# A six-stage transformer kernel on one core: attention's bias products over 128 rows of the array, ranks and transposed rows taken one unit sooner

## The chip, the core and the metric

The kernel runs on one core of one Trainium2 chip. The core has a matmul engine (TensorE, "PE"; its weight loads are "PEld"), a vector engine (VectorE, "DVE"), a scalar engine (ScalarE, "ACT"), GpSimd ("POOL") and SyncE ("SP"), which here only issues DMAs. They run apart from one another and meet at semaphores. The metric is the device time of one execution in microseconds; lower is better.

## The reference

The input is x of shape 16 x 256 x 128, 4096 tokens of width 128. Six stages follow, each added to x. The one that the change touches is the second, a differential attention with 16 heads of width 8, two maps each:

```
x = x + 0.5 * ffn(layernorm(x))          # experts, top 2 of 8
x = x + attn(layernorm(x))               # the stage of the change
x = x + 0.5 * ffn(layernorm(x))          # experts again
x = x + 0.5 * quantized_ffn(layernorm(x))
x = x + linear_attention(layernorm(x))
x = x + 0.5 * quantized_ffn(layernorm(x))

attn: q = x @ Wq.T + bq; k = x @ Wk.T + bk; v = x @ Wv.T + bv; rope on q1, q2, k1, k2
      a1 = softmax(causal(q1 k1 * scale)); a2 = softmax(causal(q2 k2 * scale))
      out = (a1 - lam * a2) @ v, divided by its root mean square, times head_norm_w and 0.8
      return out @ Wo.T + bo
```

The third stage sorts tokens by expert. Its routing of a group of 512 tokens (normalise, transpose, router product, the two best experts, the rank of each token within its expert, the row it is sent to) is done inside the attention, for all groups but the last of eight.

## The kernel before

All of x stays in SBUF, as 32 tiles of 128 tokens. `diff_attention` works on 16 blocks of two tiles (256 tokens) in 19 turns, which this text numbers 0 to 18. In turn t, block A = t is projected and packed, block B = t-1 gets its scores for the row maxima, block C = t-2 its transposed scores, exponentials and value products, and block D = t-3 its division, normalisation and output product. A turn has 24 units u; each engine's program is written out unit by unit, and this order alone sets what runs when, as no scheduler moves anything. Between engines there are semaphores and buffers of two or six.

What the text refers to:

- In each unit PE computes `scores(B, u)` into one of two banks `s_ps` (L2202, L2205, L2210) and `scores_T(C, u)` into one of two banks `st_ps` (L2227). DVE takes the row maximum of `s_ps` (L1933, "the maximum of unit u"); PE may write scores of unit u only after the maximum of unit u-2. ACT takes the exponential of `st_ps` into `prob` (L1784), POOL clears its upper triangle (L1719, "select"), and in every second unit PE multiplies by the values with 32 columns of weights (L2250).
- Bias products: the bias is added by a matmul of its own, whose stationary operand `two_ones` has ones in rows 0 and 32 and zeros elsewhere, and whose moving operand holds the bias in its leading 16 bits in row 0 and the rest in row 32. For q, k and v (L2371) it stands in units 7 and 10, ahead of three projection matmuls (L2373), twice in each of these units (256 and 384 columns): "a pair". For the output product it stands in unit 15 (L2398), ahead of `wo` (L2399), twice.
- `m_ps`, two banks, is shared by all the small transposes and products, so PE's later users of it wait for the readers of the earlier. In unit 5 PE transposes `oT` into it (L2353); DVE then divides (L1941, L1944), squares and sums in unit 6 (up to L1957). POOL raises the sums to the power -1/2 (L1686, twice, units 7 and 8), DVE multiplies by it in unit 10 (L2132).
- Rope: DVE multiplies the projections by cosine and sine (L1970, L1972) in units 8 and 11, POOL adds the two (L1741, "rope addition") in units 9 and 12, ACT packs the result (L1838, L1841), DVE forms the low part of `k_pack` (L2164), PE transposes it (L2414) in unit 15.
- Transposed rows: in even turns from 6 to 16 PE transposes 512 normalised tokens into bank 1 of `m_ps` in unit 2 (L2268), and ACT copies them to `exp_xT` (L1805, 128 x 1024). PE's transposes of `oT` in unit 5 wait for that copy.
- Ranks: in odd turns from 7 to 17 PE computes the ranks into the same bank in unit 2 (L2283, L2285), and DVE's `take_ranks` adds them to `run` (L2040, L2042, the tile `exp_run`). PE's unit 5 waits for that too, and for `xT_lo` (L2153, unit 3 on DVE).
- POOL also sends rows to HBM by indirect DMA (L1707, "scatter"); in even turns from 8 on the first of them is in unit 5.

## Time and profile before

| | us |
|---|---|
| median of 3 runs | 1323.84 |
| lowest, highest | 1322.83, 1324.23 |
| the profiled execution | 1324.04 |
| its span in the trace | 1322.3 |

| engine | busy us | share |
|---|---|---|
| PE | 1092.7 | 83% |
| PEld | 819.8 | 62% |
| DVE | 985.9 | 75% |
| POOL | 856.6 | 65% |
| ACT | 724.3 | 55% |

A row of the timeline gives the start, the duration, engine, source line, operation, what is written and read, the sizes and a count, and in brackets how long the engine had been idle and which instruction released it. For a matmul, "64\*128 64x256" means that 64 rows and 128 columns of the array are used and 256 columns stream through. The end of a matmul is modelled: the distance between the starts of two of them tells more than their durations. In the timeline, neighbouring instructions of one group are merged (x2 and more). A brief idle time has no bracket. The granted clock of PE is 1.00 for 2.4 GHz and 0.50 for 1.2 GHz.

### The profile page before, as it was taken

To read this page: it belongs to the slowest core of one execution; us is meant where nothing else is said; L and a number is where in the kernel's file an instruction comes from. 1 tells how busy PE (TensorE), PEld (TensorE's weight loads), DVE (VectorE), ACT (ScalarE), POOL (GpSimd) and SP (SyncE) were. 2 spreads that over 40 slices of the span, in tenths; PEclk is the share of its full clock that TensorE was granted. 3 is DMA by queue.
4 is the path that set the end of the run, shared out by engine and by line. 5 is a ranking of instruction groups with operands and counts; after the bars stand their busy time and mean duration, and the time that the engine had idled before them with its cause. 6 is when DMAs were issued, how large, how long until landed. Compare 5 with 4: busy or idle time off the path is not lost. (4 is left out here: it accounts for less than half of the span.)

```text
span 1322.3 us, 32967 instructions
## 1 busy us (share of the span) xinstructions
PE 1092.7 (83%) x11805; PEld 819.8 (62%) x11805; DVE 985.9 (75%) x2554; ACT 724.3 (55%) x1311; POOL 856.6 (65%) x1033
## 2 busy tenths in 40 slices
PE   2753996389999999999999988579994988999697
PEld 1432775156666666666666665368883875777577
DVE  6872885588888888989898875378885936888672
ACT  4721554446667676667666676335662744444174
POOL 4874777225667688878787887544774315889651
PEclk9886998589999999999999999679997898999989
DMA  8113431011110011111011010143323100000001
GB/s 258 45 48 106 112 106 53 26 39 26 26 25 20 20 30 34 33 30 33 25 34 34 24 28 12 43 132 93 105 74 115 36 1 0 1 1 1 0 25 40
DMA packets 63980, 62.78 MB, mean 47 GB/s; under 512 B 11088, under 2 KB 53488, under 8 KB 63440
## 3 DMA queue, kind: packets, MB, share of 16 engines
q1 hardware_dynamic: 54384, 39.66, 11.4%
q0 software_dynamic: 9440, 21.02, 4.7%
q8 instruction: 99, 1.62, 0.5%
q14 instruction: 57, 0.47, 0.1%
HBM read 28.10 MB, written 24.17 MB: 40 GB/s over the span
## 5 line engine op out<-in xcount | busy, mean ns | idle before, releaser
L1784 ACT ACTIVATE diff_prob<-diff_st_ps 128x512 f32<-128x512 f32 x384 | 227.8, 601 | 160.9 <-PE diff_st_ps L2227 154.2
L1933 DVE TENSOR_REDUCE diff_q_pack<-diff_s_ps 128x2 f16<-128x512 f32 (+1 forms) x384 | 262.1, 692 | 63.5 <-PE diff_s_ps L2210 60.9
L1719 POOL TENSOR_SCALAR_AFFINE_SELECT diff_prob<-diff_prob 128x256 f32<-128x256 f32 (+1 forms) x384 | 188.0, 497 | 121.9 <-ACT diff_prob L1784 119.6
L431 POOL DMA_INDIRECT exp_ys<-moe_y_sb,moe_dest x156 | 152.7, 979 | 86.8 <-ACT moe_y_sb L514 54.1
L2210 PE MATMUL diff_s_ps<-diff_k_one,diff_qT 128*128 128x128 f16 (+1 forms) x1024 | 149.8, 249 | 0.0
L2227 PE MATMUL diff_st_ps<-diff_qmT,diff_k_one 128*128 128x256 f16 (+1 forms) x1024 | 147.7, 248 | 0.3 <-ACT diff_prob L1784 0.2
L2250 PE MATMUL diff_ot_ps<-diff_prob,diff_v 128*32 128x128 f32 x3072 | 125.5, 282 | 9.1 <-POOL diff_prob L1719 6.8
L507 ACT ACTIVATE moe_h_hi<-moe_h 128x512 f16<-128x512 f32 x94 | 59.2, 630 | 88.2 <-DVE moe_h L737 88.2
L1686 POOL TENSOR_TENSOR diff_rms<-diff_ms,all_neghalf 128x8 f32<-128x8 f32 x64 | 105.0, 1641 | 3.7 <-DVE diff_ms L1957 2.8
L2210 PEld LDWEIGHTS diff_s_ps<-diff_k_one,diff_qT 128*128 128x128 f16 x1024 | 90.7, 99 | 22.2 <-issue 0.7
L2250 PEld LDWEIGHTS diff_ot_ps<-diff_prob,diff_v 128*32 128x32 f32 x3072 | 73.3, 110 | 44.5 <-issue 23.3
L2551 POOL TENSOR_TENSOR lin_y<-lin_state,lin_qT 128x512 f32<-128x512 f32 x64 | 81.9, 1280 | 11.3 <-DVE lin_state L2694 8.9
L2227 PEld LDWEIGHTS diff_st_ps<-diff_qmT,diff_k_one 128*128 128x128 f16 x1024 | 83.0, 98 | 8.8 <-ACT diff_prob L1784 2.0
L2694 DVE TENSOR_TENSOR_SCAN lin_state<-lin_lam_ps,lin_kv 128x512 f32<-128x512 f32 x64 | 77.6, 1219 | 9.3 <-POOL lin_kv L2538 7.5
L414 POOL DMA_INDIRECT exp_xs<-moe_xh,exp_rows x64 | 66.8, 1044 | 23.8 <-issue 19.0
L501 ACT ACTIVATE moe_act<-moe_g_ps 128x512 f32<-128x512 f32 x94 | 55.8, 593 | 45.9 <-PE moe_g_ps L957 41.6
L2765 PEld LDWEIGHTS lin_o_ps<-last_lin_wo,lin_y 128*128 128x128 f32 x512 | 64.9, 191 | 22.1 <-POOL lin_y L2551 18.9
L2202 PE MATMUL diff_s_ps<-diff_mask,diff_ident_bf 128*128 128x256 bf16 x256 | 72.1, 282 | 7.5 <-DVE diff_q_pack L1933 5.4
L2765 PE MATMUL lin_o_ps<-last_lin_wo,lin_y 128*128 128x128 f32 x512 | 70.2, 280 | 9.0 <-POOL lin_y L2551 8.4
L737 DVE TENSOR_TENSOR moe_h<-moe_act,moe_u_ps 128x512 f32<-128x512 f32 x94 | 64.4, 686 | 15.2 <-PE moe_u_ps L957 14.3
L732 DVE TENSOR_TENSOR moe_h_lo<-moe_h,moe_h_hi 128x512 f16<-128x512 f32 x94 | 65.1, 692 | 10.2 <-ACT moe_h_hi L507 9.0
L718 DVE COPY moe_xgT<-moe_t_ps 128x512 f16<-128x512 f16 x78 | 33.0, 424 | 38.9 <-PE moe_t_ps L939 37.7
(390 smaller groups left out, 3069.8 us busy)
## 6 DMA issues: line engine op xcount, KB each, us to landing
moe_xg<-exp_xs SPq DMA_DIRECT2D x78, 130.0 KB, 2.3
diff_k_one<-diff_kT SPq DMA_DIRECT2D x128, 64.0 KB, 2.0
diff_yg<-exp_ys SPq DMA_DIRECT2D x14, 256.0 KB, 3.0
fetched_yg<-exp_ys SPq DMA_DIRECT2D x7, 512.0 KB, 3.9
exp_ys<-moe_y_sb,moe_dest POOLq DMA_INDIRECT x156
all_x<-in_x SPq DMA_DIRECT2D x4, 512.0 KB, 5.1
moe_up<-in_w SPq DMA_DIRECT2D x16, 128.0 KB, 3.9
out<-all_x SPq DMA_DIRECT2D x8, 256.0 KB, 2.3
```

The costliest lines, as they stand in the source:

```text
L431: nc.gpsimd.indirect_dma_start(out=ew.ys, out_offset=bass.IndirectOffsetOnAxis(ap=dest[:, s, j:j + 1], axis=0), in_=y_sb[:, s % YR, j], in ...
L1686: nc.gpsimd.tensor_tensor(rms[:, j, heads], ms[:, j, heads], neghalf[:, 0:8], ALU.pow).then_inc(rms_ready, 1)
L1719: nc.gpsimd.affine_select(out=pr, in_=pr, compare_op=ALU.is_ge, fill=0.0, base=0, pattern=[[0, n], [1, P]], channel_multiplier=-1).then_in ...
L1784: nc.scalar.activation(prob[:, u % RING], st_ps[:, u % 2], ACT.Exp, scale=SCALE).then_inc(exp_ready, 1)
L1933: nc.vector.tensor_reduce(q_pack[:, par, j, m0:m0 + n, 3 * HD], s_ps[:, u % 2].rearrange("p (m k) -> p m k", m=n), op=ALU.max, axis=AX.X, ...
L2202: nc.tensor.matmul(out.rearrange("p (m k) -> p m k", k=P)[:, 1::2], ident_bf[:], mask[:, 0:2], start=True, stop=False, skip_group_check=True)
L2210: last = nc.tensor.matmul(out[:, i * wd:(i + 1) * wd], qT[:, par, c, j * P:(j + 1) * P], k_one[:, par, r, c, 0:wd], start=False, stop=True ...
L2227: last = nc.tensor.matmul(st_ps[:, u % 2, i * wd:(i + 1) * wd], k_one[:, par, r, c, key * P:(key + 1) * P], qmT[:, par, c, q0:q0 + wd], st ...
L2250: last = nc.tensor.matmul(ot_ps[32 * r:32 * r + 32, c // 2, col:col + P], v[:, par, key, (m0 + i) // 2], src, start=bool(key) and c % 2 == ...
L2551: nc.gpsimd.tensor_tensor(y[:, f % RING], state[:, f % STATES], qT[:, b], ALU.mult).then_inc(y_ready, 1)
L2694: nc.vector.tensor_tensor_scan(state[:, f % STATES], lam_ps[:, b], kv[:, f % RING], 0.0, ALU.mult, ALU.add).then_inc(state_ready, 1)
L2765: last = nc.tensor.matmul(o_ps[:, b, t * P:(t + 1) * P], y[:, f % RING, t * P:(t + 1) * P], wo[:, f], start=(f == 0 and t == 0), stop=(f = ...
```

## The change

`bias_rows`, `two_ones` and `wo_rows` get 128 partitions instead of 64, and the copies that fill them cover all 128. Rows 64 to 127 of `two_ones` are cleared with the rest, so the added products are zero times the bias. `take_ranks` moves from unit 4 to unit 3 on DVE, the copy to `exp_xT` from unit 4 to unit 3 on ACT. In unit 3 `take_ranks` stands ahead of `xT_lo`. The whole diff:

```diff
@@ -1496,9 +1496,9 @@
         xn = nm.sb("xn", [P, 2, P], F32)
         xT_hi = nm.sb("xT_hi", [P, S], F16)
         xT_lo = nm.sb("xT_lo", [P, S], F16)
-        bias_rows = nm.sb("bias_rows", [2 * LO, QKV], F16)
-        two_ones = nm.sb("two_ones", [2 * LO, P], F16)
-        wo_rows = nm.sb("wo_rows", [2 * LO, P], F16)
+        bias_rows = nm.sb("bias_rows", [P, QKV], F16)
+        two_ones = nm.sb("two_ones", [P, P], F16)
+        wo_rows = nm.sb("wo_rows", [P, P], F16)
         v_new = nm.sb("v_new", [P, 2, HEADS, HD], F32)
         v = nm.sb("v", [P, 2, 2, HEADS, PACK], F32)
         by_cos = nm.sb("by_cos", [P, 2, 2 * MAPS, HD], F32)
@@ -1799,7 +1799,7 @@
                             if norms >= 2:
                                 a.wait_ge(scattered[norms % 2], norms // 2 * 2 * TG * 16)
                             nc.scalar.activation(ew.xh[:, norms % 2, :, 0:P], n_xn[:], ACT.Copy).then_inc(n_hi, 1)
-                    g = routes if u == 4 and places is None else norms if u == 21 and norms == routed - 1 else None
+                    g = routes if u == 3 and places is None else norms if u == 21 and norms == routed - 1 else None
                     if g is not None:
                         a.wait_ge(n_xT_in_psum, g + 1)
                         nc.scalar.activation(ew.xT[:, g].rearrange("p a n -> p (a n)"), m16[1], ACT.Copy).then_inc(n_xT_ready, 1)
@@ -1889,7 +1889,7 @@
                 once(nc.vector.memset(two_ones[:], 0.0))
                 for row in (0, LO):
                     nc.vector.memset(two_ones[row:row + 1], 1.0)
-                once(nc.vector.tensor_copy(bias_rows[:], qkv_bias[0:2 * LO]))
+                once(nc.vector.tensor_copy(bias_rows[:], qkv_bias[:]))
                 nc.vector.tensor_tensor(bias_rows[LO:2 * LO], qkv_bias[LO:2 * LO], bias_rows[LO:2 * LO],
                                         ALU.subtract).then_inc(prepared, 1)
 
@@ -1904,7 +1904,7 @@
                 nc.vector.tensor_copy(ident_bf[:], ident[:])
                 nc.vector.tensor_copy(mask[:], later.causal[:].unsqueeze(1).broadcast_to([P, 4, P]))
                 nc.vector.tensor_scalar(wo[:], later.diff_wo[:], head_w[:, 0:1], 1.0 - LAMBDA_INIT, ALU.mult, ALU.mult)
-                once(nc.vector.tensor_copy(wo_rows[:], wo_bias[0:2 * LO]))
+                once(nc.vector.tensor_copy(wo_rows[:], wo_bias[:]))
                 nc.vector.tensor_tensor(wo_rows[LO:2 * LO], wo_bias[LO:2 * LO], wo_rows[LO:2 * LO], ALU.subtract)
                 if routed:
                     nc.vector.memset(going[:, :, 1:], 1.0)
@@ -2073,7 +2073,7 @@
 
                 if u == 0:
                     mark_either(g)
-                if u == 4:
+                if u == 3:
                     take_ranks(g)
                 if u == 5:
                     place_pairs(g)
```

In the preparation on DVE, in turn 0, the names are the three widened operands and the biases as loaded:

```order
-L1889 MEMSET diff_two_ones 64x64
+L1889 MEMSET diff_two_ones 128x64
 L1891 MEMSET diff_two_ones 1x128 x2
-L1892 CAST diff_bias_rows<-later_qkv_bias 64x640
+L1892 CAST diff_bias_rows<-later_qkv_bias 128x640
 L1893 TENSOR_TENSOR diff_bias_rows<-later_qkv_bias,diff_bias_rows 32x640
```

Three instructions (the third is L1907) cover twice the partitions; none is added. PE's order is the same throughout, with 128 rows in L2371 and L2398.

On ACT, around unit 3 of turn 6 (and of every even turn up to 16), `diff_xT_hi` is the projection's input, `diff_oT` the copied value products, `diff_prob` the exponentials and `exp_xT` the transposed rows:

```order
 L1813 ACTIVATE diff_xT_hi<-diff_m_ps 128x256
 L1779 ACTIVATE diff_oT<-diff_ot_ps 128x512
-L1784 ACTIVATE diff_prob<-diff_st_ps 128x512 x2
+L1784 ACTIVATE diff_prob<-diff_st_ps 128x512
 L1805 ACTIVATE exp_xT<-diff_m_ps 128x1024
-L1784 ACTIVATE diff_prob<-diff_st_ps 128x512 x5
+L1784 ACTIVATE diff_prob<-diff_st_ps 128x512 x6
```

The copy passes the exponential of unit 4.

On DVE, around unit 3 of turn 7 (and of the later odd turns), `diff_q_pack` is written by the maxima, and `exp_xh` and `diff_placed` by the step that follows the ranks:

```order
 L2113 COPY diff_oT<-diff_ot_ps 128x512
 L1933 TENSOR_REDUCE diff_q_pack<-diff_s_ps 128x2
-L2153 TENSOR_TENSOR diff_xT_lo<-diff_m_ps,diff_xT_hi 128x256
-L1933 TENSOR_REDUCE diff_q_pack<-diff_s_ps 128x2
 L2040 TENSOR_TENSOR diff_base<-diff_m_ps,exp_run 128x32
 L2042 TENSOR_TENSOR exp_run<-exp_run,diff_m_ps 128x8
-L1933 TENSOR_REDUCE diff_q_pack<-diff_s_ps 128x2
+L2153 TENSOR_TENSOR diff_xT_lo<-diff_m_ps,diff_xT_hi 128x256
+L1933 TENSOR_REDUCE diff_q_pack<-diff_s_ps 128x2 x2
 L2045 TENSOR_REDUCE exp_xh<-diff_rest 128x4
 L2047 TENSOR_TENSOR diff_placed<-diff_chosen,diff_base 128x64
```

The two instructions on the ranks pass one maximum and `xT_lo`.

## Rows read from the trace of the kernel before

**Rows 1.** the page's first part: busy us, share of the span, instructions

```profile
PE 1092.7 (83%) x11805; PEld 819.8 (62%) x11805; DVE 985.9 (75%) x2554; ACT 724.3 (55%) x1311; POOL 856.6 (65%) x1033
```

**Rows 2.** busy us of each engine in turn 8, granted PE clock, DMA

```profile
494.60:530.20 35.60, 33.08 (x455) 23.49 (x456) 30.82 (x71) 23.96 (x43) 27.53 (x40) 1.00 0.12 32
```

**Rows 3.** PE timeline, turn 8, unit 10: start us, us, operation

```profile
...
509.22 0.28 PE L2371 MATMUL diff_m_ps<-diff_bias_rows,diff_two_ones 64*128 64x256 f16 x1
509.43 0.28 PE L2373 MATMUL diff_m_ps<-diff_wqkv_hi,diff_xT_hi 128*128 128x256 f16 x1
509.55 0.27 PE L2373 MATMUL diff_m_ps<-diff_wqkv_lo,diff_xT_hi 128*128 128x256 f16 x1
509.66 0.27 PE L2373 MATMUL diff_m_ps<-diff_wqkv_hi,diff_xT_lo 128*128 128x256 f16 x1
509.87 0.33 PE L2371 MATMUL diff_m_ps<-diff_bias_rows,diff_two_ones 64*128 64x384 f16 x1
510.13 0.34 PE L2373 MATMUL diff_m_ps<-diff_wqkv_hi,diff_xT_hi 128*128 128x384 f16 x1
510.31 0.33 PE L2373 MATMUL diff_m_ps<-diff_wqkv_lo,diff_xT_hi 128*128 128x384 f16 x1
...
```

**Rows 4.** releasers of the `oT` transposes L2353: us, times

```profile
...
  ACT exp_xT L1805: 3.5, 6
  DVE exp_run L2042: 3.2, 5
...
```

**Rows 5.** ACT timeline, turn 8, units 3 to 6

```profile
...
499.53 1.14 ACT L1784 ACTIVATE diff_prob<-diff_st_ps 128x512 f32<-128x512 f32 x2
500.57 1.02 ACT L1805 ACTIVATE exp_xT<-diff_m_ps 128x1024 f16<-128x1024 f16 x1
...
503.50 0.60 ACT L1784 ACTIVATE diff_prob<-diff_st_ps 128x512 f32<-128x512 f32 x1 [1.41 <-PE diff_st_ps L2227]
...
```

**Rows 6.** DVE timeline, maximum of unit 6 in turns 6, 9, 15, 16

```profile
...
433.34 0.70 DVE L1933 TENSOR_REDUCE diff_q_pack<-diff_s_ps 128x2 f16<-128x512 f32 x1 [0.60 <-PE diff_s_ps L2210]
...
538.81 0.68 DVE L1933 TENSOR_REDUCE diff_q_pack<-diff_s_ps 128x2 f16<-128x512 f32 x1
...
750.03 0.70 DVE L1933 TENSOR_REDUCE diff_q_pack<-diff_s_ps 128x2 f16<-128x512 f32 x1 [0.66 <-PE diff_s_ps L2210]
...
784.84 0.70 DVE L1933 TENSOR_REDUCE diff_q_pack<-diff_s_ps 128x2 f16<-128x512 f32 x1 [1.49 <-PE diff_s_ps L2210]
...
```

**Rows 7.** POOL timeline, turn 8, units 3 to 12

```profile
...
501.83 1.09 POOL L1719 TENSOR_SCALAR_AFFINE_SELECT diff_prob<-diff_prob 128x512 f32<-128x512 f32 x2
...
504.47 1.07 POOL L1707 DMA_INDIRECT exp_xs<-exp_xh,exp_rows  x1 [0.18 <-issue]
...
508.33 1.62 POOL L1686 TENSOR_TENSOR diff_rms<-diff_ms,all_neghalf 128x8 f32<-128x8 f32 x1
...
510.30 1.25 POOL L1741 TENSOR_TENSOR diff_by_cos<-diff_by_cos,diff_by_sin 128x512 f32<-128x512 f32 x1
...
514.14 1.27 POOL L1741 TENSOR_TENSOR diff_by_cos<-diff_by_cos,diff_by_sin 128x512 f32<-128x512 f32 x1 [0.92 <-DVE diff_by_sin L1972]
...
```

**Rows 8.** timeline, L2132 on DVE and L1741 on POOL, turns 4, 5, 8

```profile
...
371.20 1.26 POOL L1741 TENSOR_TENSOR diff_by_cos<-diff_by_cos,diff_by_sin 128x512 f32<-128x512 f32 x1
371.48 1.26 DVE L2132 TENSOR_TENSOR diff_osq<-diff_o,diff_rms 128x256 f32<-128x256 f32 x1
...
405.83 0.52 DVE L2132 TENSOR_TENSOR diff_osq<-diff_o,diff_rms 128x256 f32<-128x256 f32 x1
...
406.05 1.44 POOL L1741 TENSOR_TENSOR diff_by_cos<-diff_by_cos,diff_by_sin 128x512 f32<-128x512 f32 x1
...
510.35 1.85 DVE L2132 TENSOR_TENSOR diff_osq<-diff_o,diff_rms 128x256 f32<-128x256 f32 x1
...
```

**Rows 9.** DVE timeline behind bias pairs, turns 0 and 2

```profile
...
250.97 0.69 DVE L1970 TENSOR_TENSOR diff_by_cos<-diff_m_ps,later_rope_cos 128x512 f32<-128x512 f32 x1 [3.12 <-PE diff_m_ps L2373]
...
299.60 0.70 DVE L1933 TENSOR_REDUCE diff_q_pack<-diff_s_ps 128x2 f16<-128x512 f32 x1 [1.02 <-PE diff_s_ps L2210]
...
```

## The prediction, made before the changed kernel was run

> **What bounds the kernel now.** The page's first part gives the largest busy share to TensorE (PE) [rows 1], but that is a mean over six stages and the change lies in one of them, the attention of 240 to 852 us. Its 19 turns are numbered 0 to 18 here; turns 3 to 15 hold all four blocks and last about 35 us each. In turn 8 PE is busy for 33.08 of 35.60 us and VectorE (DVE) for 30.82 us, at a granted clock of 1.00, the 2.4 GHz level [rows 2]; the other full turns look alike. Neither bounds the whole turn, so I read the timeline of both engines beside each other. From unit 16 of a turn to unit 5 of the next, DVE and ScalarE (ACT) wait for PE. From unit 6 to unit 15 PE waits for DVE, or GpSimd (POOL) is late. A saving on PE is kept only where DVE next waits for PE.
>
> **Part 1, bias products over 128 rows.** The matmuls keep their columns; only the row count goes from 64 to 128. In [rows 3] equal full-array matmuls of 256 columns start 0.12 and 0.11 us apart (509.43, 509.55, 509.66). The 256-column bias matmul of 64 rows holds the next one off for 0.21 us (509.22 to 509.43), a full matmul holds the second bias matmul off for 0.21 us (509.66 to 509.87), and the 384-column bias matmul holds its successor for 0.26 us where its equal takes 0.18 (510.13 to 510.31). So each change between 64 and 128 rows costs PE about 0.10 us, and a pair of bias matmuls holds three that can go: 0.3 us. The change into the first stays wherever a 32-column value product stands ahead, or is hidden in a wait. The output product (unit 15) has four, 0.4 us. There are 32 pairs and 16 output products: 9.6 + 6.4 = 16.0 us of PE, of which most lies where PE waits anyway. Bounds for one change: 0, if the row count is not what holds the successor, and 0.10 us. I take 0.10, since the same pair shows the gap on both sides of the bias matmul. The one-time copies and the clearing on DVE cover more partitions but no more elements in each; I cost them at nothing.
>
> The Trainium skill (TensorEngine Tiling, Key Properties) says that changing the tiling mode drains TensorE; by that, the trace agrees. It gives no price there. TensorE: Matmul & The Clock Gate (Single matmul latency) puts the part of a lone matmul that does not depend on its columns at 398 cycles of 2.4 GHz, an estimate of 0.17 us for an exposed drain; a pair would then save 0.5 us and the whole sum would be some 1.5 us more. The 0.10 us of the rows decides.
>
> Where a pair's 0.3 us is kept: turn 0, where DVE waits 3.12 us for the second pair [rows 9], 0.4 us at the slower clock there; both pairs of turn 1, 0.6; turn 2, where DVE waits 1.02 us after the pair of unit 7 [rows 9], 0.3. The output product is bare in turn 16 (0.3) and in the last turn (0.35). In turns 3 to 15 the maximum of unit 8 waits some 0.2 us for PE's scores behind the pair of unit 7, but that gain meets POOL below. The output product in those turns is followed by the k_pack transposes, which wait for DVE: nothing.
>
> **Part 2, transposed rows one unit sooner (even turns 6 to 16).** ACT copies `exp_xT` at 500.57, for 1.02 us, behind two exponentials [rows 5]. PE's transposes of `oT` in unit 5 wait for it: 3.5 us in 6 turns [rows 4]. The copy now goes between the two exponentials and ends about 0.55 us sooner. The second exponential, that of unit 4, then ends 1.0 us later, at about 501.7. PE needs it for scores_T of unit 6. The exponential of unit 6 starts on that product's end, at 503.50 [rows 5]; 0.58 us sooner and less about 0.4 us for the product, scores_T would start at 502.5, so 0.8 us are to spare. POOL works on the two selects of units 3 and 4 from 501.83 [rows 7], and reaches the second at about 502.4, later than 501.7 too. So the delay costs nothing; with both covers gone it would cost up to 1.0 us a turn. What is late next: in turn 6 DVE waits 0.60 us for PE at the maximum of unit 6, in turn 16 it waits 1.49 us [rows 6]. Both keep 0.58 us: 1.2 us together. In turns 8, 10, 12 and 14 POOL has a scatter of 1.07 us in unit 5 and no wait for another engine ahead of the second power (508.33 to 509.95) and the rope addition at 510.30 [rows 7]: it runs by its own length. PE's and DVE's lead of 0.4 to 0.9 us (0.2 to 0.58 from the copy, 0.2 to 0.3 from the pair) does not move that POOL work. It moves DVE's L2132 against the rope addition L1741, and the two disturb each other [rows 8]: started 0.05 us after L1741, L2132 takes 1.85 us; 0.28 us after, 1.26 us; 0.22 us before, 0.52 us. With its lead L2132 waits only for the second power (509.95) and gets in ahead of 510.30. DVE's chain is then over 1 us sooner, and what ends it next is POOL, which waits 0.92 us for DVE before its second rope addition [rows 7]. I take that whole wait as the gain, 0.9, 0.9, 0.9 and 0.7 us in the four turns (the last has the shortest such wait): 3.4 us. Bounds: 0, if L2132 still falls behind L1741, and 1.3 us a turn.
>
> The Trainium skill (Advanced Engine Details and Errata, GPSIMD Details) says that GpSimd shares a read and a write interface with VectorE, in conflict with its instructions of two SBUF inputs. L2132 has two such inputs; by that, the trace agrees, and the rows give the price that the page lacks.
>
> In turns 3 and 4 L2132 starts 0.28 us after L1741 [rows 8]. The 0.2 us that the pair gives there brings it to some 0.08 us after, where 1.85 us stands instead of 1.26: the end is tied to L1741, and I count a loss of 0.35 us each, 0.7 us. Turn 5 has L2132 ahead already and gains 0.2. Turn 6 could fall either way: 0.
>
> **Part 3, ranks one unit sooner (odd turns 7 to 17).** PE's unit 5 waits 3.2 us in five turns for `exp_run` [rows 4]. The two DVE instructions (0.18 and 0.16 us) now stand ahead of `xT_lo`, which is 0.36 us later within its unit but still ahead of the maximum of unit 4; its end then releases PE, some 0.6 us sooner. But in turn 9 the maximum of unit 6 starts at 538.81 with no wait for PE [rows 6], right behind DVE's own work, and turns 7, 11 and 13 are alike: nothing is kept. In turn 15 no fetched tile is added, DVE waits 0.66 us [rows 6], and 0.6 us is kept. Turn 17 has no such PE wait. No wait, DMA or queue of SP moves; POOL's order is unchanged.
>
> **The sum.** Starts 0.4 + 0.6 + 0.3 = 1.3; turns 3 to 6 -0.7 + 0.2 = -0.5, and 0.58 for turn 6; turns 8 to 14 3.4; turn 15 0.6; turn 16 0.58 + 0.3; turn 18 0.35. Together 6.6 us. Against the profiled execution of 1324.04 us (span 1322.3) that is 1317.4; this execution lies 0.2 us above the median of 1323.84, so 1317.2, rounded to 1317.3.
>
> **The rivals.** (a) L2132 does not get ahead of L1741 in the four turns, because what DVE wins is used up before unit 10. For it: POOL's own work does not move. Against: the lead is 0.4 us or more and 0.05 us is enough. It costs the 3.4 us: 1320.7; with half of the terms of turns 6, 15 and 16 (2.1 us) gone too, 1321.7. (b) PE bounds more than I read: the whole 16.0 us and the 6.7 us of unit 5 are kept, 1301; half of them kept gives 1312.5. Against: PE's waits for DVE between units 11 and 15. (c) The row change does not shorten the gaps (the part does not do what it says): 2.15 us of starts, ends and turn 5 go and the 0.7 us loss too, 1318.7. (d) Slower: the new timing puts L2132 within 0.09 us after L1741 in all full turns. The place is unit 10, the price 0.59 us where 1.26 stands now (7 turns) and 1.35 us where about 0.5 stands (2 turns): 6.8 us, and the 3.4 us never come. Against 3.2 us of other gains that is 3.6 us slower, 1327.4. It decides at the start of L1741: a start just after it is dear, one just before it is cheap. Against: the second power ends 0.35 us ahead of L1741.
>
> **How the numbers follow.** Forecast 0.50; (a) 0.27, two thirds of it with the further losses; (b) 0.10, nearly all in its halved form; (c) 0.07; (d) 0.06. A measurement of this kernel tells about 0.2% from no change; the bound is 1321.2 us. Faster by more: 0.50 + 0.09 of (a) + 0.10 + 0.07 = 0.76; within 0.2%: the 0.18 left of (a); slower: 0.06. The range reaches over (c), nearly all of (a) and about the halved (b): 1311.0 to 1322.0. It leaves out (d), the full (b) and the tail of (a).
>
> **What would show it.** Bias matmuls of 128 rows with successors 0.11 and 0.17 us behind them; no PE wait at the transposes of unit 5 for `exp_xT` or `exp_run`; L2132 near 0.5 us in turns 8 to 14 and near 1.8 in turns 3 and 4; odd turns 7 to 13 as long as before, even turns 8 to 14 about 0.9 us shorter. The forecast is wrong if the even turns do not shrink, or if the odd ones shrink as well.

## The result, and the profile after

The changed kernel takes 1319.34 us (median of 8 runs, 1316.73 to 1322.09) beside 1324.03 us of the kernel before (8 runs, 1322.75 to 1324.86): ratio 0.997, interval 0.9961 to 0.9978, so 3 to 5 us faster. The forecast was 1317.3 us with a range of 1311.0 to 1322.0. The page's first part, to set beside [rows 1]:

```profile
PE 1070.2 (81%) x11758; PEld 821.9 (62%) x11805; DVE 986.0 (75%) x2554; ACT 725.3 (55%) x1311; POOL 857.2 (65%) x1033
```

PE's modelled busy time falls by 22 us (47 of its 11805 records are missing here) and no other engine's changes by over 2.1 us; the kernel kept some 4. PE's timeline of the bias pair in turn 8, unit 10 (start us, us, operation), beside [rows 3]:

```profile
506.96 0.27 PE L2371 MATMUL diff_m_ps<-diff_bias_rows,diff_two_ones 128*128 128x256 f16 x1
507.06 0.27 PE L2373 MATMUL diff_m_ps<-diff_wqkv_hi,diff_xT_hi 128*128 128x256 f16 x1
...
507.28 0.27 PE L2373 MATMUL diff_m_ps<-diff_wqkv_hi,diff_xT_lo 128*128 128x256 f16 x1
507.39 0.33 PE L2371 MATMUL diff_m_ps<-diff_bias_rows,diff_two_ones 128*128 128x384 f16 x1
507.55 0.33 PE L2373 MATMUL diff_m_ps<-diff_wqkv_hi,diff_xT_hi 128*128 128x384 f16 x1
```

The bias matmuls hold their successors off for 0.10 and 0.16 us, where [rows 3] had 0.21 and 0.26, and the full matmul ahead of the second one holds it off for 0.11. The three gaps of 0.10 us are gone. In the output product of the same turn the four gaps that could go gave 0.48 us together. What L2353 waits for, beside [rows 4] (us, times):

```profile
  issue: 1.7, 6
  DVE diff_oT L2113: 1.5, 1
  DVE diff_logits L2020: 1.1, 1
```

`exp_xT` and `exp_run` no longer stand there. So parts 1, 2 and 3 do at their own places what they say. Turn 8 as a window, beside [rows 2], 35.30 us; from the first L2300 of one turn to that of the next it is 35.30 against 35.52 before:

```profile
493.00:528.30 35.30, 31.67 (x451) 23.50 (x454) 30.90 (x71) 23.88 (x43) 27.79 (x40) 1.00 0.12 32
```

PE works 1.41 us less there and the turn is 0.22 us shorter. L2132 on DVE and L1741 on POOL, in turns 3, 5 and 8 of the changed kernel, beside [rows 8]:

```profile
336.25 1.48 DVE L2132 TENSOR_TENSOR diff_osq<-diff_o,diff_rms 128x256 f32<-128x256 f32 x1
336.19 1.27 POOL L1741 TENSOR_TENSOR diff_by_cos<-diff_by_cos,diff_by_sin 128x512 f32<-128x512 f32 x1
...
405.31 0.61 DVE L2132 TENSOR_TENSOR diff_osq<-diff_o,diff_rms 128x256 f32<-128x256 f32 x1
405.62 1.44 POOL L1741 TENSOR_TENSOR diff_by_cos<-diff_by_cos,diff_by_sin 128x512 f32<-128x512 f32 x1
...
508.44 1.92 DVE L2132 TENSOR_TENSOR diff_osq<-diff_o,diff_rms 128x256 f32<-128x256 f32 x1 [0.21 <-POOL diff_rms L1686]
508.75 1.27 POOL L1741 TENSOR_TENSOR diff_by_cos<-diff_by_cos,diff_by_sin 128x512 f32<-128x512 f32 x1
```

In turn 8 L2132 gets its lead of 0.31 us, as forecast, and takes 1.92 us, not 0.5. In turn 5 the same lead gives 0.61.

The table has the stretches of the profiled executions, us. A turn runs from its first L2300 to the next turn's; turns 0 and 1 from the first L2313, 17 and 18 to the first L972, the experts from there to the last L972, the rest to the end of the span. "odd" is turns 7, 9, 11, 13 together, "even" 8, 10, 12, 14. The runs marked * were made on a chip on which the stages ahead of and behind the attention are longer (the kernel before takes 1417.47 us there); their attention turns are to be compared all the same, since the turns without a change agree to 0.05 us. Of the runs without a mark, before again and the three kernels with L2132 in unit 11 were made on one chip, the changed kernel again and parts 1, 2 and 3 alone on another.

| kernel | 0–1 | 2 | 3–5 | 6 | odd | even | 15 | 16 | 17–18 | experts | rest |
|---|---|---|---|---|---|---|---|---|---|---|---|
| before | 50.65 | 31.34 | 102.52 | 34.93 | 140.04 | 141.80 | 34.73 | 31.11 | 46.88 | 145.0 | 323.1 |
| before, again | 51.54 | 31.34 | 102.48 | 34.93 | 140.04 | 141.77 | 34.73 | 31.11 | 46.16 | 144.5 | 323.0 |
| changed | 50.94 | 30.94 | 102.10 | 34.29 | 139.44 | 141.05 | 36.22 | 30.56 | 43.76 | 147.2 | 323.3 |
| changed, again | 49.55 | 30.93 | 102.08 | 34.29 | 139.38 | 143.10 | 34.65 | 30.56 | 43.86 | 144.8 | 322.6 |
| part 1 alone | 49.77 | 30.93 | 102.06 | 34.76 | 139.39 | 145.01 | 34.70 | 30.62 | 43.76 | 147.2 | 323.6 |
| part 2 alone | 50.33 | 31.35 | 102.51 | 34.58 | 140.04 | 140.85 | 34.72 | 32.26 | 44.16 | 147.2 | 323.3 |
| part 3 alone | 50.35 | 31.34 | 102.53 | 34.93 | 140.63 | 141.93 | 34.66 | 31.12 | 44.01 | 145.2 | 323.0 |
| L2132 in unit 11 | 49.77 | 30.93 | 101.16 | 33.73 | 138.59 | 138.78 | 34.69 | 30.72 | 45.63 | 147.1 | 323.3 |
| and odd scatters | 49.66 | 30.93 | 101.60 | 33.93 | 138.52 | 138.68 | 34.14 | 30.18 | 45.86 | 146.8 | 322.6 |
| and unit-5 scatter | 49.61 | 30.92 | 101.12 | 33.73 | 138.41 | 135.53 | 34.12 | 29.94 | 44.92 | 144.7 | 322.6 |
| parts 1 and 2 * | 50.10 | 30.94 | 102.11 | 34.48 | 139.45 | 143.14 | 34.72 | 30.56 | 44.50 | | |
| L1741 in unit 10 * | 49.80 | 30.20 | 100.35 | 33.62 | 139.20 | 146.65 | 34.66 | 30.56 | 44.26 | | |
| odd scatters * | 49.26 | 30.93 | 102.11 | 34.30 | 140.06 | 142.56 | 33.47 | 30.56 | 45.15 | | |
| both * | 49.66 | 30.20 | 99.74 | 33.61 | 136.53 | 148.89 | 33.49 | 30.56 | 44.72 | | |

### The profile page after: what moved, and what is told of

The parts are those of the page before. It is cut to its first block and busy times, and to the rows that moved or that the text cites. A ratio compares the mean times of both kernels' runs of the same rounds, so it can differ in the third digit from the quotient of the medians.

```text
span 1319.7 us, 32920 instructions
## 1 busy us (share of the span) xinstructions
PE 1070.2 (81%) x11758; PEld 821.9 (62%) x11805; DVE 986.0 (75%) x2554; ACT 725.3 (55%) x1311; POOL 857.2 (65%) x1033
## 5 line engine op out<-in xcount | busy, mean ns | idle before, releaser
L2227 PE MATMUL diff_st_ps<-diff_qmT,diff_k_one 128*128 128x256 f16 (+1 forms) x1024 | 147.2, 247 | 0.3 <-ACT diff_prob L1784 0.2
L2250 PEld LDWEIGHTS diff_ot_ps<-diff_prob,diff_v 128*32 128x32 f32 x3072 | 73.3, 110 | 45.9 <-issue 21.1
```

Of the source, the lines that this page charges most:

```text
L2227: last = nc.tensor.matmul(st_ps[:, u % 2, i * wd:(i + 1) * wd], k_one[:, par, r, c, key * P:(key + 1) * P], qmT[:, par, c, q0:q0 + wd], st ...
L2250: last = nc.tensor.matmul(ot_ps[32 * r:32 * r + 32, c // 2, col:col + P], v[:, par, key, (m0 + i) // 2], src, start=bool(key) and c % 2 == ...
```

## The experiments

### The changed kernel again, and the kernel before again

> The changed kernel once more, for a second profile of it on another run of the chip. What is asked: does turn 15 again lose about 1.5 us against the kernel before, with PE waiting 1.8 us ahead of the k_pack transposes L2414 at unit 15 and its granted clock at 0.50 in the 2 us behind it, and does turn 17 again run at 1.00 where the kernel before ran at 0.50? If the fall of the clock belongs to the program (theory: the wait of 1.8 us is long enough by itself), both come again, turn 15 at 36.2 us and the whole at 1319.3 plus or minus 1. If it is a matter of where the chip happens to look (rival), turn 15 comes out at about 34.7 us in this profile and the runs spread over 5 us again.

Measured: 1319.71 us (6 runs). Turn 15 took 34.65 us, so the loss of the first profile did not come again; turns 10 and 14 were 0.7 and 1.5 us longer than in the first profile instead. Turn 14 is thus one kernel in one turn on two executions. PE is the same up to its wait for `by_sin` in unit 13; here are windows of 2 us (PE, PEld, DVE, ACT, POOL busy, granted clock, DMA), the changed kernel first, then again:

```profile
722.00:724.00 2.00, 1.38 (x27) 1.12 (x29) 1.96 (x5) 1.41 (x4) 1.28 (x1) 1.00 0.00 0
724.00:726.00 2.00, 1.88 (x29) 1.44 (x29) 1.54 (x4) 2.00 (x5) 0.64 (x1) 1.00 0.03 8
```

```profile
724.00:726.00 2.00, 1.80 (x21) 1.56 (x21) 1.40 (x4) 1.92 (x5) 1.33 (x2) 0.54 0.00 0
726.00:728.00 2.00, 2.00 (x28) 1.28 (x25) 1.32 (x4) 2.00 (x5) 0.84 (x2) 0.61 0.03 8
```

Behind the same two waits of PE (1.15 us for DVE's maximum, 0.62 us for `by_sin`) the clock stayed at 1.00, the 2.4 GHz level, in one execution and fell to 0.5, the 1.2 GHz level, in the other. The falls shown here stand behind such waits, but the same waits come without a fall too. The expected theory that the wait of 1.8 us in turn 15 is enough by itself is wrong: it came again, 1.83 us at L2414, and the clock stayed at 1.00. The experts' stage shows the same: 32 to 48 us into it the clock was 0.69 and 0.88 in the first profile and 0.79 and 1.00 in the second, and the stage took 147.2 and 144.8 us:

```profile
881.20:889.20 8.00, 6.36 (x47) 5.29 (x48) 7.62 (x23) 2.39 (x4) 0.00 (x0) 0.69 0.50 119
889.20:897.20 8.00, 8.00 (x93) 7.46 (x92) 6.76 (x19) 3.48 (x6) 0.00 (x0) 0.88 0.21 51
```

```profile
882.70:890.70 8.00, 7.54 (x70) 6.59 (x71) 7.63 (x24) 1.98 (x4) 0.00 (x0) 0.79 0.47 116
890.70:898.70 8.00, 7.95 (x99) 7.15 (x97) 7.73 (x22) 3.99 (x8) 0.00 (x0) 1.00 0.29 69
```

> The kernel before once more, for a second profile. From the first L2300 of turn 17 to the first L972 behind the attention the profile of before has 46.92 us; the profiles of the changed kernel, of it again, and of parts 1, 2 and 3 alone have 43.81, 43.86, 43.76, 44.16 and 44.0. If the missing 3 us are one execution's fall of the granted clock (0.50 through 825 to 830 us), as part 3 alone says, which hardly differs from before there, this profile shows about 44 us and a clock of 0.9 or more in that stretch, with the turns before it as in the first profile to 0.1 us. If the change gained them (rival), it shows 46.9 again. On whatever chip it runs, the turns' lengths are to be the same to 0.1 us, except where the clock fell.

Measured: 1323.78 us (11 runs), ratio 0.9995 (0.9986 to 1.0004). Turns 17 and 18 took 46.16 us, against 46.88 in the first profile. That is not the 44 us of the theory, and it is not clearly the rival either: the twelve profiles of other kernels lie between 43.8 and 45.9, and the three of them that were made on the same chip as this one have 45.63, 45.86 and 44.92, while the four on the chip of parts 1, 2 and 3 have 43.76 to 44.16. Those three kernels differ from the changed one in these turns too, so the chip's part in it is not separated. In before's two profiles, in the changed kernel's two and in part 3 alone PE waits 2.7 us for POOL's select in turn 17 and the clock falls to 0.50 at about that wait. PE then runs at 1.2 GHz for some 10 and 7 us in before's two profiles, for some 3 us in the changed kernel's first and in part 3 alone, and for some 7 us, the first of them within the wait, in the changed kernel's second, which took 43.86 us all the same. Before, two windows:

```profile
820.00:826.00 6.00, 4.65 (x49) 3.25 (x49) 1.30 (x2) 3.13 (x7) 5.62 (x9) 0.56 0.05 14
826.00:832.00 6.00, 6.00 (x54) 4.08 (x54) 2.17 (x6) 2.32 (x5) 2.88 (x6) 0.58 0.07 22
```

and part 3 alone, whose work is the same there up to that wait:

```profile
821.40:827.40 6.00, 4.67 (x53) 3.40 (x54) 1.30 (x2) 3.10 (x7) 5.62 (x9) 0.72 0.05 14
827.40:833.40 6.00, 5.65 (x96) 3.76 (x93) 3.27 (x9) 4.46 (x8) 5.47 (x9) 1.00 0.10 33
```

Part 3 alone, which saves nothing ahead of that wait, has the gain too, so the saved work does not make it. What sets the length of the low clock stays open, and so does whether more executions would keep before and the others apart.

### Each part alone

Part 1 alone (against the changed kernel):

```diff
-                    g = routes if u == 3 and places is None else ...
+                    g = routes if u == 4 and places is None else ...
...
-                if u == 3:
+                if u == 4:
                     take_ranks(g)
```

> Part 1 alone: bias matmuls over 128 rows, transposed rows and ranks at unit 4 as before. By the prediction's own terms: starts 1.3, turns 3 to 5 -0.5, ends 0.65, and of the four even turns nothing or little: 1.5 to 2.2 us faster than before. What the trace of after suggests instead: turns 0 to 2 1.1 us, turns 3 and 4 nothing (L2132 takes 1.48 us there, not 1.85), the last three turns up to 3 us of clock and gaps: 2.5 to 4 us faster, so that this part alone carries most of the 4.7 us. Rival (PE bounds all): 16 us faster or a good part of it. The bias matmuls must show successors 0.11 and 0.17 us behind them, and PE's waits for exp_xT (3.5 us a turn) and exp_run (3.2) in unit 5 must still be there, 0.3 to 0.5 us longer.

Measured: 1325.46 us (12 runs) beside 1323.53 (29 runs), ratio 1.0011 (1.0 to 1.0023): no gain at all, for the part that saves PE 16 us. In its profile turns 0 to 2, 3 to 5, the odd turns and the last two did gain (by the table 1.7, 0.4, 0.65 and 2.8 us against the mean of before's two), and the even turns gave 3.2 back, the experts 2.5. PE's waits in unit 5 are still there, 3.5 us for `exp_xT` and 3.2 for `exp_run`. Turn 12:

```profile
649.35 3.03 DVE L2132 TENSOR_TENSOR diff_osq<-diff_o,diff_rms 128x256 f32<-128x256 f32 x1
...
649.16 0.40 POOL L1719 TENSOR_SCALAR_AFFINE_SELECT diff_prob<-diff_prob 128x256 f32<-128x256 f32 x1
649.53 1.26 POOL L1741 TENSOR_TENSOR diff_by_cos<-diff_by_cos,diff_by_sin 128x512 f32<-128x512 f32 x1
650.76 1.34 POOL L1719 TENSOR_SCALAR_AFFINE_SELECT diff_prob<-diff_prob 128x256 f32<-128x256 f32 x3
654.32 1.27 POOL L1741 TENSOR_TENSOR diff_by_cos<-diff_by_cos,diff_by_sin 128x512 f32<-128x512 f32 x1 [2.23 <-DVE diff_by_sin L1972]
```

L2132 starts 0.18 us ahead of L1741, within a select, and ends at 652.38, 0.28 us behind the three selects (650.76 to 652.10) that follow L1741. It was held off through five POOL instructions, four of which started after it. PE then waits for DVE's maximum, and its clock falls:

```profile
653.05 0.28 PE L2202 MATMUL diff_s_ps<-diff_mask,diff_ident_bf 128*128 128x256 bf16 x1 [1.95 <-DVE diff_q_pack L1933]
```

```profile
654.00:656.00 2.00, 1.61 (x25) 1.31 (x29) 1.88 (x4) 1.73 (x5) 1.27 (x1) 0.81 0.00 0
656.00:658.00 2.00, 2.00 (x24) 1.40 (x25) 1.32 (x5) 2.00 (x6) 0.70 (x2) 0.50 0.03 8
```

Turn 12 is 1.67 us longer than before, turn 14, where L2132 takes 3.03 us again, 2.01. In turns 8 and 10 L2132 starts 0.01 us behind L1741, takes 1.53 us, and the turns gain 0.24 us each.

Part 2 alone (the kernel before with `u == 3` in ACT's copy of `exp_xT`):

> Part 2 alone: exp_xT copied in unit 3 of the even turns, bias products over 64 rows and ranks at unit 4 as before. By the prediction: turns 6 and 16 keep 0.58 us each, turns 8 to 14 gain up to 0.9 each if the lead of about 0.4 us brings L2132 ahead of L1741: 1.2 to 4.6 us faster. By the trace of after (a lead of 0.31 us did not shorten L2132, it took 1.92 us and ended 0.34 us behind L1741): 0.58 us in turns 6 and 16 and 0 to 0.15 in turns 8 to 14: 1.0 to 1.6 us faster. Rival: the second exponential, 1.0 us later, is waited for by POOL's select and PE's scores_T, and the turns get up to 0.5 us longer: 0 to 3 us slower.

Measured: 1321.91 us (12 runs), ratio 0.999 (0.998 to 0.9999): 1.6 us, just clear of no change. Turn 6 keeps 0.35, the even turns 0.95 together, and turn 16 loses 1.15: there L2132 stands beside POOL's selects alone, no L1741 is near. Part 2 first, then part 3 alone, turn 16:

```profile
790.28 1.92 DVE L2132 TENSOR_TENSOR diff_osq<-diff_o,diff_rms 128x256 f32<-128x256 f32 x1 [1.48 <-POOL diff_rms L1686]
...
790.22 1.70 POOL L1719 TENSOR_SCALAR_AFFINE_SELECT diff_prob<-diff_prob 128x256 f32<-128x256 f32 x4
```

```profile
792.92 0.61 DVE L2132 TENSOR_TENSOR diff_osq<-diff_o,diff_rms 128x256 f32<-128x256 f32 x1 [1.28 <-POOL diff_rms L1686]
...
792.86 1.89 POOL L1719 TENSOR_SCALAR_AFFINE_SELECT diff_prob<-diff_prob 128x256 f32<-128x256 f32 x4
```

Both L2132 start 0.06 us behind the first select. Once, in part 3 alone, DVE gets in behind the first select, and POOL's four selects take 0.19 us more; once, in part 2, it waits for all four. So the selects too, not the rope addition alone, shut it out.

Part 3 alone (the kernel before with `u == 3` ahead of `take_ranks`):

> Part 3 alone: ranks taken in unit 3 of the odd turns, bias products over 64 rows and transposed rows at unit 4 as before. By the prediction odd turns 7 to 13 keep nothing and turn 15 keeps 0.6 us: 0.6 us faster, no difference that can be measured. Rival: PE's wait of 3.2 us for exp_run is what holds the odd turns, then each of five gives up to 0.6 us: 3 us faster. Second rival: xT_lo, 0.36 us later, or the changed distance at the k_pack transposes of turn 15 costs: turn 15 longer by up to 1.5 us because PE idles 1.8 us there and its granted clock falls; if this part makes that, turn 15 is 36.2 us here, and 34.7 us in the kernel with part 1 alone.

Measured: 1323.72 us (11 runs), ratio 1.0002 (0.9993 to 1.001). Odd turns 7, 9 and 11 are as before to 0.01 us, turn 15 is 0.07 shorter; turn 13 is 0.58 longer in this profile, because DVE's L1926 waits 0.19 us for the DMA that fetches `diff_yg` and it and its neighbours then run later and longer. PE's shorter wait is given to DVE's own work, as the prediction had it for the odd turns.

Parts 1 and 2 without 3 (the changed kernel with `u == 4` ahead of `take_ranks`):

> The change without its third part: bias products over 128 rows and transposed rows in unit 3, ranks in unit 4 as before. Part 1 alone was 1.9 us slower than before in the median, with L2132 at 3.03 us in turns 12 and 14 (it had started 0.18 us ahead of L1741), part 2 alone 1.6 us faster, part 3 alone 0.2 us slower; their sum is 0.5 us slower, the whole change 4.3 us faster. Theory (part 2's lead moves L2132 in the even turns from 0.18 us to 0.31 us ahead of L1741, where it takes 1.92 us, and so takes part 1's loss away): 1318.5 to 1320.5, L2132 at 1.92 us in turns 8 to 14, and part 3 is worth nothing here either. Rival (part 3 is what makes up the difference): 1323 or more, with L2132 at 3.03 us in one or more of the even turns, or with odd turns 7 to 13 0.3 us longer than in the changed kernel.

Measured, on the other chip: ratio 0.9958 (0.9942 to 0.9975), 7 runs. L2132 takes 1.91 us in all four even turns, starting 0.31 us ahead of L1741, and of turns 2 to 16 none but turn 6 (34.48 for 34.29) and turns 10 and 14 (35.90 and 36.68 us, to 0.01 us as in the changed kernel's second profile, where the clock fell) differs from the changed kernel's undisturbed ones by over 0.1 us. Theory right: part 3 is worth 0.3 us at most, and parts 1 and 2 together are worth more than their sum, since part 2's lead moves L2132 from where it takes 3.03 us to where it takes 1.9.

### The price of the meeting

POOL's first rope addition one unit later (against the changed kernel):

```diff
-                        if u in (9, 12):
-                            j = (u - 9) // 3
+                        if u in (10, 12):
+                            j = (u - 10) // 2
```

> The changed kernel with one more edit: POOL does its first rope addition (L1741, 1.27 us) behind the select of unit 10 instead of unit 9, so that DVE's multiply L2132 no longer meets it. It measures the disputed cost by itself. Theory (the meeting of L2132 with L1741 is what uses up the lead of DVE and PE): L2132 takes 0.42 to 0.65 us in every turn instead of 1.28 to 1.93; turns 8, 10, 12 and 14 get up to 0.74 us shorter (that is POOL's wait for DVE before its second rope addition, which then ends the stretch), turns 3, 4 and 6 up to 0.8; odd turns 7 to 13 little, since POOL's second rope addition stands behind a scatter of 1.08 us there and does not wait for DVE: 3 to 6 us faster than the changed kernel, 1313 to 1316. Rival (POOL, or PE between units 11 and 15, bounds those units in all turns whatever L2132 does): no turn changes by over 0.1 us, 1319.3. Second rival: the first rope addition, 0.4 us later, delays ScalarE's k_pack and q_pack copies and PE idles longer before L2414: slower than the changed kernel by up to 0.4 us a turn.

Measured: ratio 0.9967 (0.9951 to 0.9983), that of the changed kernel, so no gain. By turns, against the changed kernel: 0.9 us gained in turns 3 and 4 each and 0.67 in turn 6, where L2132 now takes 0.60 us instead of 1.48; nothing in turn 5, where it had 0.61 before; 0.24 in each of turns 7, 9 and 13 (turn 11 is 0.5 longer, with DVE waiting for `diff_yg`); and 3.6 to 5.6 lost in the even ones together, the falls of the clock in turns 10 and 14 included. Turn 2, which has no L2132, gained 0.73 too, so L1741's place has a worth of its own and the price of the meeting is not measured cleanly. In the even turns L2132 starts 0.67 us ahead of L1741 and takes 2.57 us, through two selects, L1741 and the select behind it. The theory fails there: even a lead of 0.67 us is not enough.

The scatters of the odd turns later:

```diff
-    SEND_AT = {0: (10, 13, 16, 18, 19, 20, 22, 23), 4: (5, 16, 18, 20)}
+    SEND_AT = {0: (13, 16, 18, 19, 20, 21, 22, 23), 4: (5, 16, 18, 20)}
```

> The changed kernel with the scatters that POOL issues in odd turns moved from units 10, 13, 16, 18 to units 13, 16, 18, 19 (in turn 17 eight of them from 10 to 23 to 13 to 23), so that no scatter of 1.08 us stands ahead of its second rope addition. Theory on turn 15 (PE waits 1.83 us before L2414 because POOL's second rope addition is late behind the scatter; that wait lets the granted clock fall to 0.50 and costs 1.5 us): the wait falls to about 0.8 us, the clock stays at 1.00 through 760 to 768 us, turn 15 takes 34.7 us or less instead of 36.2. Odd turns 7 to 13, where L2164 waits 0.45 us for the k_pack copy behind that rope addition: up to 0.45 us shorter each. Together up to 3 us faster than the changed kernel, 1316.5. Rival (odd turns are bounded by DVE's own work there, and the fall of the clock comes with the wait at another place): within 0.5 us of 1319.3.

Measured: ratio 0.9976 (0.9961 to 0.9992), so the whole shows no gain over the changed kernel. Turn 15 takes 33.47 us, 1.2 less than the 34.65 of the undisturbed profile of the changed kernel. PE's wait in unit 15 there, the changed kernel and then this one:

```profile
761.22 0.91 PE L2414 MATMUL diff_m_ps<-diff_ident_h,diff_k_pack 128*128 128x128 f16 x8 [1.83 <-DVE diff_k_pack L2164]
```

```profile
809.59 0.62 PE L2414 MATMUL diff_m_ps<-diff_ident_h,diff_k_pack 128*128 128x128 f16 x8 [0.72 <-DVE diff_k_pack L2164]
```

So turn 15 is held by POOL's scatter of 1.08 us ahead of its second rope addition. Odd turns 7 to 13 gained nothing (140.06; turn 13 was 0.6 longer, with the same wait for `diff_yg` as in part 3 alone): rival right there.

Both edits:

> Both edits on the changed kernel: first rope addition in unit 10, scatters of the odd turns from unit 13 on. If L2132's meeting with L1741 (1.28 us instead of 0.5) and the scatter are two covers of the same stretch in the odd turns, each alone gives the odd turns little and both together give up to 0.7 us in each of turns 7, 9, 11, 13: 1310 to 1314 in all, faster than the sum of the two runs alone. If PE or DVE's other work bounds the odd turns, this is the sum of the two.

Measured: ratio 0.9944 (0.9924 to 0.9964), against 0.9967 and 0.9976. The odd turns fall to 136.53 us, 0.7 a turn below the changed kernel, where the edits alone gave 0.24 a turn and nothing: two covers of one stretch, as expected, that is, two pieces of work side by side, of which each hides most of what taking the other away would save. The even turns are at 148.89, so the whole misses the 1310 to 1314 that was expected (0.9944 would be 1316.6). There L2132 takes 2.57 us, PE waits 1.80 us for DVE, and the clock falls, turn 8:

```profile
548.45 2.57 DVE L2132 TENSOR_TENSOR diff_osq<-diff_o,diff_rms 128x256 f32<-128x256 f32 x1 [0.22 <-POOL diff_rms L1686]
```

```profile
551.69 0.28 PE L2202 MATMUL diff_s_ps<-diff_mask,diff_ident_bf 128*128 128x256 bf16 x1 [1.80 <-DVE diff_q_pack L1933]
```

```profile
550.00:552.00 2.00, 0.31 (x3) 0.29 (x4) 2.00 (x3) 0.00 (x0) 1.51 (x3) 1.00 0.00 0
552.00:554.00 2.00, 1.38 (x21) 1.12 (x20) 2.00 (x5) 1.08 (x3) 1.03 (x1) 0.69 0.00 0
554.00:556.00 2.00, 2.00 (x23) 1.26 (x21) 0.88 (x3) 2.00 (x6) 0.87 (x2) 0.50 0.00 0
```

### L2132 behind the meeting instead of ahead of it

Against the changed kernel, in DVE's program:

```diff
                     if D is not None:
-                        if u == 10:
+                        if u == 11:
                             dve.wait_ge(rms_ready, D * 4 + 4)
```

> The changed kernel with DVE's multiply L2132 taken in unit 11 instead of 10, behind that unit's maximum and ahead of the rope products; everything else, L1741's place too, stays. Theory (L2132 ends 0.28 us behind L1741 whenever it meets it, and what counts is what it holds up meanwhile): it starts 0.6 to 0.9 us later, takes 0.7 to 1.0 us and ends where it ended, but the maximum of unit 11 (0.6 us) is no longer held up behind it. So DVE's rope products and POOL's second L1741 come 0.6 us sooner: turns 3, 4, 6, 8, 10, 12 and 14 get 0.4 to 0.6 us shorter, odd turns 7 to 13 up to 0.2, since a scatter stands ahead of POOL's second L1741 there: 2.5 to 4.5 us faster than the changed kernel. Rival (POOL does not let L2132 in before its selects are through, as in part 1 alone, where it took 3.03 us, and with L1741 moved, 2.57 us): it takes 1.5 us or more in turns 8, 10, 12 and 14, these turns get longer, up to 1.9 us where PE's wait lets the granted clock fall to 0.50, and the whole is slower than the changed kernel.

Measured: 1316.07 us (5 runs), ratio 0.9927 (0.9914 to 0.9941): below the changed kernel by 3.6 us in the medians, by 5.3 in the ratios (0.9967 there). The even turns are 0.5 to 0.6 us shorter than the changed kernel's, the odd ones 0.2, turn 6 is 0.56, turns 3 and 4 0.6 and 1.0; turn 5, where L2132 had got in and now takes 1.05, is 0.66 longer. Theory right on the turns; L2132 takes 1.18 us in the even ones, where 0.7 to 1.0 was expected, and ends 0.34 us behind L1741. Turn 8:

```profile
507.98 1.18 DVE L2132 TENSOR_TENSOR diff_osq<-diff_o,diff_rms 128x256 f32<-128x256 f32 x1
...
507.56 1.26 POOL L1741 TENSOR_TENSOR diff_by_cos<-diff_by_cos,diff_by_sin 128x512 f32<-128x512 f32 x1
```

With the odd scatters later as well:

> The same with the scatters of the odd turns from unit 13 on. With L1741 moved and the scatters too, odd turns 7 to 13 were 0.83 to 0.90 us shorter than before, with the scatters alone 0.15. Theory: the two hold the same stretch of the odd turns, so this one has them 0.7 to 0.9 us shorter than before (0.6 to 0.7 shorter than the changed kernel), and even turns as in the run with L2132 in unit 11 alone: 5 to 7 us faster than the changed kernel. Rival (L2132's place is not what L1741's move was): odd turns 0.15 us shorter than before, and no more than 1.5 us in all over the run with L2132 in unit 11 alone, all of it in turn 15, whose wait before L2414 goes.

Measured: 1315.61 us (5 runs), ratio 0.9923 (0.9909 to 0.9936). The rival holds: the odd turns stay at 138.52, and the whole is the same as in the run before; turns 15 and 16 gain 0.55 us each, turns 4 and 6 lose 0.4 and 0.2. L2132 takes 0.68 us in the odd turns and ends 0.64 behind L1741, which itself stands where it stood; with both edits it took 0.41 ahead of an L1741 one unit later. Which of the two the odd turns' 2 us hang on was not tried.

And the scatter of unit 5 in the even turns later, `4: (16, 18, 19, 20)`:

> And the scatter of unit 5 in the even turns moved behind unit 16 too (units 16, 18, 19, 20 instead of 5, 16, 18, 20), so that POOL's two powers and its first rope addition come 1.08 us sooner there. Theory (in the even turns POOL's own work from unit 3 to unit 9 sets when L2132 may start): even turns 8 to 14 up to 0.9 us shorter than in the run without this edit, 1 to 3.5 us in all. Rival (the prediction's row: DVE and PE are next in line by 0.2 to 0.6 us): L2132 starts earlier but the turns gain 0.3 us or less, or, with POOL's selects in one piece behind it, L2132 takes 2.5 us or more again and they lose.

Measured: 1308.37 us (4 runs, 1308.03 to 1309.13), ratio 0.9878 (0.9863 to 0.9893). This version beats both kernels, by 16 and 11 us. The even turns fall from 138.68 to 135.53, 0.8 us each; theory right. In this run L2132 meets only the last 0.12 us of L1741 and POOL is 1.08 us sooner, both at once; which of the two gives the 0.8 us was not tried. Turn 8, with L2132 at 0.41 us:

```profile
507.32 0.41 DVE L2132 TENSOR_TENSOR diff_osq<-diff_o,diff_rms 128x256 f32<-128x256 f32 x1
...
506.17 1.27 POOL L1741 TENSOR_TENSOR diff_by_cos<-diff_by_cos,diff_by_sin 128x512 f32<-128x512 f32 x1
```

```profile
491.10:525.10 34.00, 31.86 (x455) 23.48 (x455) 29.39 (x72) 23.92 (x43) 27.66 (x40) 1.00 0.13 33
```

Turn 8 is 1.6 us shorter than before with the same work. The whole gained more than the even turns: of the 9.3 us between the two profiles 3.2 lie in them, 2.1 in the experts' stage (144.7 for 146.8), 1.9 ahead of the attention, 1.0 in turns 17 and 18, and 0.7 in turns 4 and 6. What the edit does there, if anything, is not shown; in the experts' stage it is the clock's matter again.

## Why the prediction was right, and where it was not

The time came within 2.1 us of the forecast and inside the range, but half of its sum did not happen, and other terms took its place. It lies nearer to rival (a), 1320.7, than to the forecast, and my own sign of being wrong came true: the even turns hardly shrank, and the odd ones shrank as well. "Gain" is the change against the two profiles of before.

**Row changes, 0.10 us each.** Right, to 0.01 us in the pairs; the output product gave 0.12 for each.

**Starts, 1.3 us.** Turn 2 gains 0.40 in every profile, for 0.3. Turns 0 and 1 gain 0.9 us in the mean of two profiles each, for 1.0, but the profiles of one kernel differ there by 0.9 and 1.4 us; over all, the ten with part 1 have 49.26 to 50.94, the four without it 50.33 to 51.54, and the means are 0.9 apart. So this term is supported, not shown.

**"With its lead L2132 ... gets in ahead", 3.4 us.** This step failed. L2132 got the lead and took 1.92 us. The even turns gained 0.22, 0.29, 0.16 and 0.08 us, 0.75 together, in the first profile (and lost 1.3 in the second, where the clock fell). I read [rows 8] as a matter of which instruction starts first, from turn 5, where a start 0.22 us ahead gave 0.52 us; a row of that kind in an even turn did not exist. Rival (a) named the outcome for another reason, that the lead would be used up. What ends DVE's chain there is POOL's work after all: with L2132 behind L1741 (unit 11) the even turns are 0.5 to 0.6 us shorter, and with the scatter gone too 0.8 more.

**Turns 3 to 6, -0.7 and +0.2.** The place was right (a start 0.06 us behind L1741) and the size wrong: 1.48 us, not 1.85, because L2132 ends 0.28 us behind L1741 there, whether it starts 0.28 us behind it, as before, or 0.07. The price is set by the end, so being earlier costs nothing. Turns 3 and 4 stayed as they were, and turn 5 gained 0.4 (0.2 forecast): 0.4 us instead of a loss of 0.5. The 1.85 of turn 8 in [rows 8], ending 0.65 us behind, was taken from an even turn for turns 3 and 4. Rival (d) counts their 0.7 us twice, in its 6.8 and in the 3.2 of other gains; without that it is 1326.7, outside the range as well.

**Turn 6, 0.58.** 0.64 measured; 0.17 from part 1 and 0.35 from part 2 alone.

**Ranks.** Nothing in odd turns 7 to 13: right. The 0.15 us that each of them gains is there in part 1 alone (139.39) and is PE's saving, which I had put at zero. Turn 15 was to keep 0.6 and kept 0.08, or lost 1.5 with the clock: what was late next there is POOL's rope addition behind its scatter, which I had not looked for.

**Turn 16, 0.88.** 0.55 measured, of which 0.49 came with part 1 alone, for 0.3; of the 0.58 from the copy 0.06 is left, and alone it lost 1.15.

**Last turns, 0.35.** 2.7 measured in the mean of two profiles each. No term for it was in the sum, nor for the experts' stage, where the second of two lengths 2.4 us apart came up in one profile of two. Their sum has both signs. The two kernels had the longest and nearly the shortest last turns of all that were profiled, and no run shows that the change makes the difference; it may be the clock's chance, or partly the chip's. Falls of the clock of 1.5 us and two lengths of the experts' stage are also a reason for runs of one kernel to differ (by 5.4 us in 8 runs of the changed kernel, 7.3 in 12 of part 1 alone, 4.5 in 29 of the kernel before), but that they make these spreads is argued, not shown: the mean granted clocks of the runs follow their times only loosely (0.923 in the run of 1321.44 us, 0.922 in that of 1316.73).

So in turns 0 to 16 the sum of 6.3 us became 4.3 where no clock fell (0.9 and 0.4 in turns 0 to 2, 0.4 in 3 to 5, 0.6 in 6, 0.6 in the odd turns, 0.75 in the even ones, 0.1 and 0.55 in 15 and 16). Falls of the clock took back 1.6 us in the one profile and 2.1 in the other, turns 17 and 18 gave 2.7, and the experts' stage and the stretch ahead of the attention took 1.2 and 1.1 in the mean. The profiled executions are 2.6 and 3.1 us faster, the medians 4.7. That the measured time is close to the forecast is in good part luck.

What the traces show of the two engines together is simpler than a race. L2132 runs 224 times in the 14 profiles. The last one of each profile has no POOL instruction beside it and takes 0.42 or 0.43 us; the other 210 all end 0.27 to 0.36 us behind the end of a POOL instruction. What differs is which one. In 152 it is the one that runs when L2132 starts: a select (0.41 to 0.69 us, as in turn 5, where the select ends 0.33 us after the start; this is what "gets in" comes to) or L1741 (up to 1.49 us). In the other 58 it is one that starts with or after L2132: L1741 (1.53 to 1.93 us), the select behind L1741 (0.67 to 1.85 us, the last in turn 8 of before, and 2.57 us with L1741 in unit 10), the last of four selects (1.92 us, part 2 in turn 16) or the third select behind L1741 (3.03 us, part 1 alone). In turn 5 and turn 8 of the changed kernel the three starts agree to 0.01 us (POOL's select, L1741 and L2132 at 405.24, 405.62, 405.31 and 508.38, 508.75, 508.44), and the durations are 0.61 and 1.92. That L2132 had waited for POOL's power in turn 8 does not decide it: in turn 15 it had too, with starts alike to 0.02 us, and took 0.61. Both profiles of the changed kernel have the same in every turn, to 0.02 us; those of before do but for turns 12 and 14, with 1.81 and 1.53 in one and 1.53 and 1.82 in the other. The Trainium skill (SBUF — State Buffer, Who interferes with whom) states that a VectorE instruction with two SBUF inputs contends with a GpSimd instruction that reads SBUF, that the port pair they share is an exclusive lock, and that the order of issue decides who blocks. That L2132 waits for the end of a POOL instruction agrees with the trace (210 of 224 times). The order of issue does not account for which one: 3.03, 2.57 and 1.92 us were held through instructions that started after L2132. What decides that is not settled; no run here separates it.

## What to carry to other kernels

A saving on an engine that waits elsewhere moves the others against each other, so ask of each pair of engines which instructions will now run at the same moment; parts 1 and 2 were worth -1.9 and 1.6 us alone, and the ratio of both together was 0.9958, 3 to 8 us. Where two engines obstruct each other, do not try to win the race by a few tenths of a microsecond: put work that the other does not obstruct there (the maximum of unit 11 ahead of L2132, 3.6 us in the medians) or take away what makes the other late (a scatter of 1.08 us, 0.8 us in each of four turns). And where a stretch has two covers, taking one away shows nothing; take both in one run (nothing and 0.24 us a turn alone, 0.7 together).

## What was not expected of the hardware

- DVE's multiply of 128x256 values takes 0.41 us at its shortest and up to 3.03 us beside POOL, through five POOL instructions in a row. Beside POOL it ended 0.27 to 0.36 us behind the end of one of POOL's instructions 210 times out of 210.
- PE's clock fell to 1.2 GHz behind waits of 1.15 and 0.62 us in one execution and stayed at 2.4 GHz in another of the same kernel; the fall in turn 14 or 15 cost some 1.5 us of the turn.
- At the same wait of 2.7 us in turn 17 the low clock lasted some 3, 7 or 10 us in different executions, 3 and 7 us in the two of the changed kernel, and turns 17 and 18 were 2.7 us longer in before's two profiles than in the changed kernel's: over half of what the whole change measured, and not shown to be the change's.
